# Edge loop of a graph layer: the runs' copy placed between two tiles' old rows, and high and low parts side by side in one product of 16 columns

## What is computed

```python
# gnn part of the reference: n = 1250 nodes, e = 20000 edges sorted by dst, 8 heads of 64
x_cat = jnp.concatenate([node_feat[src], node_feat[dst], edge_feat], axis=-1)
r = x_cat @ Wr.T + br
q = (node_feat @ Wq.T + bq).reshape(n, H, D)
k = (r @ Wk.T + bk).reshape(e, H, D)
v = (r @ Wv.T + bv).reshape(e, H, D)
a = jnp.einsum('ehd,ehd->eh', q[dst], k) * scaler
amax = jax.ops.segment_max(a, dst, num_segments=n)
ae = jnp.exp(a - amax[dst])
asum = jax.ops.segment_sum(ae, dst, num_segments=n)
attn = ae / asum[dst]
m = v * attn[..., None]
out = jax.ops.segment_sum(m, dst, num_segments=n).reshape(n, H * D)
...
x = x + gnn(layernorm(x), ...) + linear_attention(layernorm(x), ...)
x = x + quantised_ffn(layernorm(x), ...)
```

## Time and profile before

| | |
|---|---|
| median of 3 runs | 1622.1 us (1619.85 to 1623.33) |
| profiled execution | 1626.55 us, its span 1624.8 us |
| edge loop within the span | about 278 to 1395 us |
| PE busy | 1551.1 us, 95% |
| PEld busy | 1202.1 us, 74% |
| DVE busy | 1256.3 us, 77% |
| ACT busy | 1054.6 us, 65% |
| POOL busy | 694.3 us, 43% |

### The profile page before, as it was taken

One profiled execution on the slowest core, in us unless ns is written; L12 is line 12 of the kernel. 1 busy time (PEld: TensorE's weight loads), 2 busy tenths in 40 slices (PEclk: granted clock), 3 DMA queues, 4 the chain that ended last, 5 costly groups with the idle time before them and its releaser, 6 DMA issues. The chain is left out here.

```text
span 1624.8 us, 27304 instructions
## 1 busy us (share of the span) xinstructions
PE 1551.1 (95%) x7334; PEld 1202.1 (74%) x7334; DVE 1256.3 (77%) x3141; ACT 1054.6 (65%) x3706; POOL 694.3 (43%) x722
## 2 busy tenths in 40 slices
PE   7999898999999999999999999999999999899996
PEld 6786676777777777777777777777777777777673
DVE  5866664887788778788788778878877878678878
ACT  3785122677777777777777777777777777567245
POOL 1001123556555555555555565555555565211001
PEclk9999999999999999999999999999999999999997
DMA  6575414666666666666676666666666666175001
GB/s 194 180 247 181 174 67 137 200 215 202 210 208 207 224 211 216 211 199 199 201 239 218 198 218 204 211 206 212 220 208 209 202 201 198 45 236 192 27 14 51
DMA packets 135446, 300.31 MB, mean 185 GB/s; under 512 B 34863, under 2 KB 56502, under 8 KB 135296
## 3 DMA queue, kind: packets, MB, share of 16 engines
q0 software_dynamic: 63600, 180.17, 33.6%
q1 hardware_dynamic: 66512, 107.59, 22.2%
q10 hardware_dynamic: 5184, 10.81, 1.8%
HBM read 271.40 MB, written 66.58 MB: 208 GB/s over the span
## 5 line engine op out<-in xcount | busy, mean ns | idle before, releaser
L1110 ACT ACTIVATE wv<-vv,expd 128x64 f32<-128x64 f32 x1248 | 314.6, 334 | 2.7
L1122 ACT ACTIVATE old<-old,expd 128x64 f32<-128x64 f32 x1232 | 302.1, 334 | 0.0
L1032 POOL DMA_INDIRECT merge<-new,put_id x157 | 162.8, 1037 | 269.2 <-DVE new L1453 236.9
L1882 PE MATMUL psK<-M_hi,efT_hi 128*128 128x512 f32 x628 | 254.3, 405 | 2.8 <-ACT efT_hi L1080 2.8
L1882 PE MATMUL psV<-M_hi,efT_hi 128*128 128x512 f32 x628 | 256.1, 408 | 0.0
L1883 PE MATMUL psK<-M_lo,efT_hi 128*128 128x512 f32 x628 | 250.0, 398 | 0.0
L1883 PE MATMUL psV<-M_lo,efT_hi 128*128 128x512 f32 x628 | 249.5, 397 | 0.0
L1003 POOL DMA_INDIRECT old<-merge,dst_id x157 | 157.8, 1005 | 142.6 <-DMA merge<-new,put_id 116.9
L1096 ACT ACTIVATE expd<-diff 128x32 f32<-128x32 f32 (+1 forms) x79 | 18.1, 229 | 289.3 <-DVE diff L1432 289.3
L1003 POOL DMA_INDIRECT kv<-kv_table,src_id x157 | 162.3, 1034 | 66.1 <-issue 47.8
L1003 POOL DMA_INDIRECT qc<-q_table,dst_id x157 | 155.0, 987 | 54.6 <-issue 46.6
(11 more groups left out here) (323 smaller groups left out, 3334.7 us busy)
## 6 DMA issues: line engine op xcount, KB each, us to landing
first_ef<-in_ef_turned_dram SPq DMA_DIRECT2D x39, 512.0 KB, 5.0
efT<-in_ef_turned_dram SPq DMA_DIRECT2D x39, 512.0 KB
merge<-empty ACTq DMA_DIRECT2D x4, 2640.0 KB, 10.0
rows<-merge SPq DMA_DIRECT2D x40, 256.0 KB, 3.7
row_block<-dst_rows POOLq DMA_DIRECT2D x13, 768.0 KB, 6.1
dst_line<-dst_rows SPq DMA_DIRECT2D x78, 128.0 KB, 2.7
end_line<-end_rows SPq DMA_DIRECT2D x78, 128.0 KB, 4.3
kv_table<-kv_out SPq DMA_DIRECT2D x10, 512.0 KB, 3.2
```

Of the source, the lines that this page charges most:

```text
L1032: pool.indirect_dma_start(out=merge[2 * (p % 2) + u][:, :], out_offset=bass.IndirectOffsetOnAxis(ap=put_id[:, t:t + 1], axis=0), in_=new[p ...
L1110: act.activation(wv[:, u, h * DH:(h + 1) * DH], vv[p % 2][:, u, h * DH:(h + 1) * DH], ACT.Copy, scale=expd[p % 2][:, u, 0, h:h + 1]).then_ ...
L1122: act.activation(rows, rows, ACT.Copy, scale=expd[p % 2][:, u, 1, h:h + 1]).then_inc(old_scaled, 1)
L1882: pe.matmul(out[:, :], efT_hi[b][:, u, c, :], Me_hi[:, c, col:col + D], start=c == 0, stop=False)
```

## The change

The scores' runs and the exponentials get one tensor each, in which the 8 columns of the high part and the 8 of the low part lie side by side. One product of 16 columns takes the place of two of 8; it leaves the two parts in 16 columns of PSUM, and a reduction on DVE adds them up (`top_sum`, `den_sum`). What waited for the maximum or the denominator only in order to have PSUM free waits for this reduction instead. `merge_den` no longer waits for `scale_den` ahead of its first operation, but ahead of its second one. On ACT, `scale_old` takes one tile at a time, and `copy_runs(p-1)` stands between the first tile and the second.

```diff
-            runs_hi = loop("runs_hi", [P, 2, H], F32R)
-            runs_lo = loop("runs_lo", [P, 2, H], F32R)
+            runs_split = loop("runs_split", [P, 2, 2, H], F32R)
+            top_sum = loop("top_sum", [P, 2, H])
...
-            exp_hi = loop_two("exp_hi", [P, 2, H], F32R)
-            exp_lo = loop_two("exp_lo", [P, 2, H], F32R)
+            exp_split = loop_two("exp_split", [P, 2, 2, H], F32R)
+            den_sum = loop("den_sum", [P, 2, H])
...
-        den = psO[:, 2 * P:2 * P + 2 * H].rearrange("p (u h) -> p u h", h=H)
+        den = psO[:, 2 * P:2 * P + 4 * H].rearrange("p (u s h) -> p u s h", s=2, h=H)
...
-        top = psT[:, 2 * H:4 * H].rearrange("p (u h) -> p u h", h=H)
+        top = psT[:, 2 * H:6 * H].rearrange("p (u s h) -> p u s h", s=2, h=H)
...
-            def scale_old(p):
-                for u in range(tiles_of(p)):
-                    act.wait_ge(old_in[p % 2], landed(p))
-                    for h in range(H):
-                        rows = old[p % 2][:, u, h * DH:(h + 1) * DH]
-                        act.activation(rows, rows, ACT.Copy, scale=expd[p % 2][:, u, 1, h:h + 1]).then_inc(old_scaled, 1)
+            def scale_old(t):
+                p, u = t // 2, t % 2
+                act.wait_ge(old_in[p % 2], landed(p))
+                for h in range(H):
+                    rows = old[p % 2][:, u, h * DH:(h + 1) * DH]
+                    act.activation(rows, rows, ACT.Copy, scale=expd[p % 2][:, u, 1, h:h + 1]).then_inc(old_scaled, 1)
...
                 if p >= 2:
-                    scale_old(p - 2)
+                    scale_old(2 * p - 4)
                 if p >= 1:
                     copy_runs(p - 1)
+                if p >= 2:
+                    scale_old(2 * p - 3)
...
             def maximum(p):
                 b, n = p % 2, tiles_of(p)
                 dve.wait_ge(top_done, 2 * p + n)
+                if p >= 1:
+                    dve.wait_ge(max_step, newmax_at(p - 1))
+                dve.tensor_reduce(top_sum[:, 0:n, :], top[:, 0:n, :, :].rearrange("p u s h -> p u h s"),
+                                  AX.X, ALU.add).then_inc(max_step, 1)
+                dve.wait_ge(max_step, top_at(p))
                 dve.wait_ge(old_in[b], landed(p))
...
-                dve.tensor_tensor(new[b][:, 0:n, ROW:TROW], old[b][:, 0:n, ROW:TROW], top[:, 0:n, :],
+                dve.tensor_tensor(new[b][:, 0:n, ROW:TROW], old[b][:, 0:n, ROW:TROW], top_sum[:, 0:n, :],
                                   ALU.max).then_inc(max_step, 1)
...
             def merge_den(p):
                 b, n = p % 2, tiles_of(p)
                 dve.wait_ge(summed, 2 * p + n)
-                dve.wait_ge(den_step, scaled_at(p))
-                dve.tensor_tensor(new[b][:, 0:n, D:ROW], den[:, 0:n, :], old_den[:, 0:n, :], ALU.add).then_inc(den_step, 1)
+                dve.tensor_reduce(den_sum[:, 0:n, :], den[:, 0:n, :, :].rearrange("p u s h -> p u h s"),
+                                  AX.X, ALU.add).then_inc(den_step, 1)
+                dve.wait_ge(den_step, den_sum_at(p))
+                dve.tensor_tensor(new[b][:, 0:n, D:ROW], den_sum[:, 0:n, :], old_den[:, 0:n, :], ALU.add).then_inc(den_step, 1)
...
-                    pe.matmul(top[:, u, :], from_end[:, u, :], runs_hi[:, u, :], start=True, stop=False)
-                    pe.matmul(top[:, u, :], from_end[:, u, :], runs_lo[:, u, :], start=False, stop=True).then_inc(top_done, 1)
+                    pe.matmul(top[:, u, :, :].rearrange("p s h -> p (s h)"), from_end[:, u, :],
+                              runs_split[:, u, :, :].rearrange("p s h -> p (s h)"), start=True, stop=True).then_inc(top_done, 1)
...
-                    pe.matmul(den[:, u, :], same[p % 2][:, u, :], exp_hi[p % 2][:, u, :], start=True, stop=False)
-                    pe.matmul(den[:, u, :], same[p % 2][:, u, :], exp_lo[p % 2][:, u, :], start=False, stop=True)
+                    pe.matmul(den[:, u, :, :].rearrange("p s h -> p (s h)"), same[p % 2][:, u, :],
+                              exp_split[p % 2][:, u, :, :].rearrange("p s h -> p (s h)"), start=True, stop=True)
```

More of the change, by code:

```diff
@@ L870, in score_at, with top_at, diff_at, scaled_at @@
             return 2 * t + 2
+        def top_at(p):
+            return 4 * p + 1
         def newmax_at(p):
+            return 4 * p + 2
+        def diff_at(p):
+            return 4 * p + 4
+        def scaled_at(p):
             return 3 * p + 1
-        def diff_at(p):
+        def den_sum_at(p):
+            return 3 * p + 2
+        def den_at(p):
             return 3 * p + 3
[L879 to L884, removed]
         def exp_at(p):
@@ L1086, in copy_runs @@
                     act.wait_ge(top_done, 2 * p)
-                act.activation(runs_hi[:, 0:n, :], turned_s[:, 0:n, :], ACT.Copy).then_inc(runs_copied, 1)
+                act.activation(runs_split[:, 0:n, 0, :], turned_s[:, 0:n, :], ACT.Copy).then_inc(runs_copied, 1)
             def weights(p):
@@ L1100, in weights_high @@
                 act.wait_ge(exp_ready, exp_at(p))
-                act.activation(exp_hi[p % 2][:, 0:n, :], expd[p % 2][:, 0:n, 0, :], ACT.Copy).then_inc(exp_ready, 1)
+                act.activation(exp_split[p % 2][:, 0:n, 0, :], expd[p % 2][:, 0:n, 0, :], ACT.Copy).then_inc(exp_ready, 1)
             def weigh_v(t):
@@ L1383, in runs_low_part @@
                     dve.wait_ge(top_done, 2 * p)
-                dve.tensor_tensor(runs_lo[:, 0:n, :], turned_s[:, 0:n, :], runs_hi[:, 0:n, :].bitcast(F32),
+                dve.tensor_tensor(runs_split[:, 0:n, 1, :], turned_s[:, 0:n, :], runs_split[:, 0:n, 0, :].bitcast(F32),
                                   ALU.subtract).then_inc(runs_low, 1)
@@ L1391, in exp_low_part @@
                     dve.wait_ge(summed, 2 * (p - 1))
-                dve.tensor_tensor(exp_lo[b][:, 0:n, :], expd[b][:, 0:n, 0, :], exp_hi[b][:, 0:n, :].bitcast(F32),
+                dve.tensor_tensor(exp_split[b][:, 0:n, 1, :], expd[b][:, 0:n, 0, :], exp_split[b][:, 0:n, 0, :].bitcast(F32),
                                   ALU.subtract).then_inc(exp_low, 1)
@@ L1907, in sort_scores @@
                     if p >= 2:
-                        pe.wait_ge(den_step, den_at(p - 2))
+                        pe.wait_ge(den_step, den_sum_at(p - 2))
                     pe.matmul(sorted_s[:, u * P:(u + 1) * P], score_hi[:, u, :], to_rank[:, u, :], start=True, stop=False)
@@ L1915, in turn_runs @@
                 if p >= 1:
-                    pe.wait_ge(max_step, newmax_at(p - 1))
+                    pe.wait_ge(max_step, top_at(p - 1))
                 for u in range(tiles_of(p)):
@@ L1935, in sums @@
                 if p >= 1:
-                    pe.wait_ge(den_step, den_at(p - 1))
+                    pe.wait_ge(den_step, den_sum_at(p - 1))
                 for u in range(tiles_of(p)):
```

## The result

The changed kernel takes 1555.27 us (median of 5 runs, 1554.38 to 1558.94), the kernel before 1622.1 us (5 runs, 1619.85 to 1623.33). The ratio is 0.9596, 95% interval 0.9582 to 0.961: 66.8 us, 4%, faster. The forecast was 1551.6 us. The profiled execution has a span of 1552.6 us.

The account below looks back on a forecast made before the run. A round between ACT and DVE of 14.26 us a pair, not PE at 13.75, was taken to bound the loop. Removing PE's stall (36 us) and 314 products (34.5 us) gave 70.5 us, from 1622.1 to 1551.6 us; range 1544 to 1580.

Parts of the forecast that it names:

- What bounds the kernel now: Edge loop: a round between ACT and DVE of 14.26 us a pair bounds it; PE's own work is 13.75 us.
- The copy between two tiles: ACT's copy_runs: 1.97 us of scalings leave the round, 0.38 us of reductions join; PE's stall goes, 36 us counted.
- One product for two: PE's spread_top and sums: 314 matmuls and weight loads fewer at 0.11 us, 34.5 us, once PE is the bound.
- The waits: PE's waits for top_at and den_sum_at bind nowhere; sort_scores' room against merge_den grows from 0.26 to over 0.8 us.
- (a): DVE's reductions cost near the upper end, so the round stays the bound: 42 us gained, 1580 us; 10%.
- (b): Gathers of old rows land late and hold DVE: up to 0.3 us a pair, 23 us, 1575 us; 10%.
- (c): PE's weight load is hidden, so a removed product saves only 0.03 us, 9.4 us in all: 1577 us; 6%.
- (d): Slower: the copy holds ACT when the runs aren't turned yet, 29 us more, 1651 us; 4%.
- What would show it: Signs: pairs 13.3 us apart, waits for copied runs gone, DVE waiting for PE's values, ACT's last-difference wait about 2.8 us.

Follow-up runs that it names:

- e1: Kernel before with only copy_runs moved between the two tiles' scale_old: 1584.5 us, ratio 0.9763.
- e2: Changed kernel with copy_runs again behind both tiles' scale_old, leaving the wide products and their reductions: 1656.92 us, ratio 1.021.
- e3: Kernel before with the first small product of sums made twice for each tile: 1625.31 us, ratio 1.0015.
- e9: Changed kernel itself, unaltered, run again as control: 1556.12 us, ratio 0.9576 to the kernel before, which took 1624.64 us beside it.
- e10: Changed kernel with six more reductions behind top_sum in maximum(p), each waiting for the one ahead: 1623.87 us, ratio 0.9999.
- e4: Changed kernel with the wide product of sums made twice for each tile: 1568.12 us, ratio 0.9656.

## Why the prediction was right

**What bounds the kernel now.** Right. The reading of a round of 14.26 us between ACT and DVE against 13.75 us of PE's own work is borne out by e1 (13.75), e2 (slower with less work for PE) and e3 (additional work for PE within 0.3%).

**The copy between two tiles.** Forecast 36 us, measured 38.2 (e1). The new round was put at 12.67 us; it is 12.75 by DVE's rows above, with the reductions at 0.18 us each and 0.21 from one to the operation that waits for it (forecast 0.19). The size was right, the path only in part: the prediction closed this round through the copy of the runs and set DVE's idle time for the high part of the exponentials aside as not needed for the sum. That idle time (0.67 us) is where the remaining round closes. DVE was free for the runs at the right moment: its wait there fell from 144.0 us to 0.6.

**One product for two.** The price was right and the sum came out smaller. Four loads at 0.11 us should bring the pair from 13.75 to 13.31 us; it is 13.30. But the step from e1 to the changed kernel is worth 1584.5 - 1556.1 = 28.4 us, not 34.5 (about 30 by the ratios to the kernel before, which took 2 us more beside e9). The missing 4 to 6 us are in the long pairs: what pairs are longer than 13.75 us in e1 adds up to 1.4 us, what they are longer than 13.30 in e9 to 6.9. So the term that was mis-sized is the gain of the products, by what the shorter pair gives back where a transfer lands late. The total came within 3.7 us of the forecast in part by luck, since the copy brought 2 us more than was counted and the products less.

**The waits.** Right as to `sort_scores`: nothing in the list waits for `den_sum`. The wait to watch was another one, that of the sums for the weighed values, of which the prediction only said that about 2 us of such waiting may stay.

**The rivals.** (a), a costly reduction, is refuted: 0.18 us. Its point of decision was good: with 1.35 us more on the round, e10 falls back onto ACT and DVE. (b), the old rows' late landing, is what happened in part. It was priced at up to 23 us as a case of its own beside the forecast; it came to 8 us within it, in six pairs and not spread over all. The margin of 0.7 us between landing and `maximum` was about right for a common pair. From the issue of the first scatter to the landing of the second gather behind it the median is 11.4 us in the kernel before and 11.7 in e9. In the pair above, `maximum` would have gone on at 515.99 - 2.49 = 513.50, which is 12.6 us after the scatter of 500.92, so a trip of 11.7 us has 0.9 us to spare; the gather of that pair landed after 15.0. So only the slowest landings held DVE, as the rival's condition (over a microsecond late) says, and the prediction, which worked from the median, had no row for how often they come. For two of the six pairs, the ones behind a load of 1 MB (`w_raw`), the profile shows what went ahead of the gather; for the others it shows the late landing, or a late issue, alone. (c), a hidden load, is refuted by e4: 0.10 us for each product. (d), a copy that holds ACT, didn't occur in the changed kernel (the turned runs were there), and the copy's place ahead of both tiles has no usable measurement.

**What would show it.** ACT's wait for the last difference was to fall to 2.8 us a pair: it is 222.2/77 = 2.9. DVE was to wait for PE's values: 33.0 us.

## What to carry to other kernels

A busy share of 95% doesn't say that an engine bounds a loop. Take the distance of two rounds of the loop where the engine doesn't wait (here at the start, before the lead of the others was used up) and compare it with the common one; if they differ, follow the waits around until they close, and look in the order of the engines for something that stands in the round without belonging there. Work taken off an engine counts only from the point at which it is the bound: the same wide products made the kernel 34 us slower alone, and 28 us faster once the copy had been moved. When a pair becomes shorter, every transfer inside it loses that time too, so ask which consumer has the least room behind the slowest landing, and put the product that waits for it later in the order.

## What was unexpected

Gathers of old rows landed 5.1 us after their issue in the median, and 8.4 at most, where the kernel before had 3.7 and 6.3. Most of this is an earlier issue and not a later arrival. `fetch_old` waits until the scatter ahead of it has landed. POOL's waits for that (300 to 1340 us) in the kernel before, the changed kernel and e1:

```profile
POOL old L1003 <- DMA merge<-new,put_id: 105.1, 69, 3.6
POOL old L1009 <- DMA merge<-new,put_id: 33.2, 21, 4.9
POOL old L1003 <- DMA merge<-new,put_id: 7.5, 7, 1.7
```

Scatters landed 3.8 us after their issue in the median before and 2.4 after, so that POOL mostly finds them landed and issues the gathers at once: the second gather 6.6 us behind the first scatter (507.53 - 500.92), where it was 7.8 in the median before. Gathers for which POOL had to wait landed 3.5 to 3.7 us after their issue in the median in both kernels; those that went out at once, 5.1 us in the changed one. The whole trip, from first scatter to second landing, is 11.4 us before, 11.7 in e9 and 12.2 in e1. So the number that grew, issue to landing, overstates what happened. Why scatters land sooner and gathers then take longer is open. The traffic grew little: the same bytes were moved in 4% less time (218 GB/s over the span, from 208), and the DMA engines' busy share in the loop went from 0.67 to 0.69.

The loops derived from the changed one were fragile across chips: of two kernels, each run on two chips, one went from 1624 to 1791 us and the other from 1551 to 1718, while the kernel before went from 1625 to 1631.
